# Self attention of a two-layer cross-attention block: scores from four 64x64 tiles, and V, staging and copy of V one place further ahead

## What is computed

```
qkv = x @ w_qkv + b_qkv
q, k, v = jnp.split(qkv, 3, axis=-1)
# mha, per batch and head (Sq = Skv = 56, D_HEAD = 8, 16 heads):
scores = einsum('bhqd,bhkd->bhqk', qh, kh) / sqrt(8)
attn = softmax(scores)
sa = einsum('bhqk,bhkd->bhqd', attn, vh)  @ w_so + b_so
x = layer_norm(x + sa, ln_g, ln_b)
```

## Time and profile before

| | |
|---|---|
| median of 3 runs | 1102.7 us (1102.0 to 1103.2) |
| the profiled execution | 1105.47 us, of which the span in the trace is 1103.7 us |
| busy share of the span | PE 93%, DVE 67%, ACT 51%, POOL 35% |
| mean granted PE clock | 0.96 of full speed |
| self attention, first matmul to the start of the last copy to att | 25.15 to 68.95 us of the span |
| what follows it | barrier, first matmul of the next block at 69.50 us |

### The profile page before, as it was taken

One profiled execution on the slowest core, in us unless ns is written; L12 is line 12 of the kernel. 1 busy time (PEld: TensorE's weight loads), 2 busy tenths in 40 slices (PEclk: granted clock), 3 DMA queues, 4 the chain that ended last, 5 costly groups with the idle time before them and its releaser, 6 DMA issues. The chain is left out here.

```text
span 1103.7 us, 31615 instructions
## 1 busy us (share of the span) xinstructions
PE 1023.4 (93%) x12044; PEld 744.2 (67%) x12044; DVE 743.7 (67%) x1406; ACT 566.9 (51%) x1135; POOL 390.1 (35%) x273
## 2 busy tenths in 40 slices
PE   4975899999999999979688999999999999999997
PEld 2652576777777776745335777787777777777786
DVE  4655778887888878320796767677677676767752
ACT  2442577776776777731345444445444444445542
POOL 4821121111211123030105554546455454555542
PEclk9986899999999999979798999999999999999998
DMA  3502544445444443030021111110111111111100
GB/s 99 143 2 91 144 133 130 134 145 148 132 132 129 146 129 91 2 98 1 1 56 43 57 56 42 51 44 33 54 56 54 47 43 55 35 40 56 35 4 4
DMA packets 47021, 79.90 MB, mean 72 GB/s; under 512 B 6978, under 2 KB 33812, under 8 KB 46964
## 3 DMA queue, kind: packets, MB, share of 16 engines
q1 hardware_dynamic: 46964, 79.10, 24.4%
HBM read 50.93 MB, written 21.96 MB: 66 GB/s over the span
## 5 line engine op out<-in xcount | busy, mean ns | idle before, releaser
L1366 ACT ACTIVATE P<-PS 125x448 f32<-125x448 f32 x384 | 207.1, 544 | 265.7 <-PE PS L1275 263.8
L1256 POOL TENSOR_TENSOR Pl<-P 125x896 f16<-125x896 f32 x128 | 230.0, 1802 | 237.4 <-ACT P L1366 237.4
L1002 DVE TENSOR_REDUCE m<-PS 128x1 f32<-128x500 f32 x336 | 220.7, 674 | 115.3 <-PE PS L993 113.4
L908 DVE TENSOR_REDUCE m_part<-PS 128x1 f32<-128x500 f32 x336 | 210.4, 673 | 60.8 <-PE PS L810 59.4
L1291 PE MATMUL PS<-cNh,P 125*128 125x97 f16 x1344 | 197.9, 208 | 0.1
L1293 PE MATMUL PS<-cNh,Pl 125*128 125x97 f16 x1344 | 197.4, 207 | 0.0
L1292 PE MATMUL PS<-cNl,P 125*128 125x96 f16 x1344 | 196.8, 206 | 0.0
L886 ACT ACTIVATE Pb<-PS 125x448 f32<-125x448 f32 x384 | 185.9, 547 | 20.1 <-PE PS L785 18.7
L1292 PEld LDWEIGHTS PS<-cNl,P 125*128 125x128 bf16 x1344 | 131.8, 98 | 25.4
L810 PE MATMUL PS<-KH,Qmx 128*128 128x500 f16 x336 | 129.7, 388 | 13.9 <-PEq L682 7.8
L1291 PEld LDWEIGHTS PS<-cNh,P 125*128 125x128 bf16 x1344 | 131.2, 98 | 15.7 <-issue 3.2
(11 more groups left out here) (167 smaller groups left out, 1521.9 us busy)
## 6 DMA issues: line engine op xcount, KB each, us to landing
Kst<-k_halves SPq DMA_DIRECT2D x144, 125.0 KB, 2.8
k_halves<-KH SPq DMA_DIRECT2D x16, 750.0 KB, 3.3
cx<-in_ctx SPq DMA_DIRECT2D x16, 562.5 KB
d_cx<-in_ctx SPq DMA_DIRECT2D x16, 562.5 KB
c_halves<-cHi SPq DMA_DIRECT2D x16, 281.2 KB, 2.6
c_halves<-cLo SPq DMA_DIRECT2D x16, 281.2 KB, 3.0
cTh<-c_halves SPq DMA_DIRECT2D x16, 281.2 KB, 3.1
cTl<-c_halves SPq DMA_DIRECT2D x16, 281.2 KB, 4.0
```

What stands on the lines that cost most here:

```text
L908: nc.vector.tensor_reduce(m_part[:, t, part:part + 1], PS[:, 6 + k % 2, 0:SP], AX.X, ALU.max).then_inc(s_reduced, 1)
L1002: nc.vector.tensor_reduce(m21[:, t, part:part + 1], PS[:, S1[k % 2], 0:SP], AX.X, ALU.max).then_inc(n_red, 1)
L1256: nc.gpsimd.tensor_tensor(Pl[:, c % NP], P1[:, c % NP], high, ALU.subtract).then_inc(n_low_p, 1)
L1366: nc.scalar.activation(P1[:, c % NP, half * HALF:(half + 1) * HALF], PS[0:KC, u % 3, 0:HALF], ACT.Exp).then_inc(n_exp, 1)
```

## The change

It has three parts.

1. Scores by halves. Heads 0 to 7 lie in feature rows 0 to 63 and heads 8 to 15 in rows 64 to 127. A half of the heads now uses only its own 64 rows of Qp and of Kbd, so a tile's four score matmuls have 64x64 weights, each in another quarter of PE's array (rows 0 or 64, columns 0 or 64), with the same 448 columns each. Kbd shrinks to 128 rows by 8x56 = 448 columns per batch (the table C_M8 has the mask r % 64 // 8), and has two slots in the same memory, so Kbd of tile t waits for the scores of tile t-2.
2. V one tile further ahead. PE makes V of tile t+1 in step t (`own_values`), in the same place, between the transposes and the product. The waits that stood before the scores of t+1 (staging, Sm of t-1, both batches of Kbd) now stand there, ahead of V of t+1, and nothing is waited for at the scores. DVE copies V2 of t ahead of top of t instead of behind Sm of t.
3. ACT stages t+1 ahead of the two copies to PT of t-1, and now also waits for the scores of t-1.

The core of the diff:

```diff
 TWO_ONES = float(np.array(0x3C003C00, np.uint32).view(np.float32))
-C_ID, C_M4, C_MM, C_M16, C_MV, C_END = 0, 128, 132, 139, 155, 157
+C_ID, C_M4, C_MM, C_M16, C_MV, C_M8, C_END = 0, 128, 132, 139, 155, 157, 165
 def shape_table():
...
     t[:, C_M16:C_MV] = r // DH0 == np.arange(H)
-    t[:, C_MV:C_END] = r // SQ == np.arange(2)
+    t[:, C_MV:C_M8] = r // SQ == np.arange(2)
+    t[:, C_M8:C_END] = r % 64 // DH0 == np.arange(8)
     return t
...
         selfa = ExitStack()
-        Kbd = sb_in(selfa, "Kbd", [D, 2, H, SQ])
+        Kbd = sb_in(selfa, "Kbd", [D, 2, 2, H // 2, SQ])
         Qp = sb_in(selfa, "Qp", [D, 2, 2, 64])
...
                                     spread(tab[:, C_M16:C_MV], 2, SQ), ALU.mult).then_inc(qmx_laid, 1)
-        def lay_own_keys(t, j):
-
-            nc.gpsimd.tensor_tensor(Kbd[:, j], SKT[:, bass.ds(t * 2 + j, 1), :].broadcast_to([D, H, SQ]),
-                                    spread(tab[:, C_M16:C_MV], 2, SQ), ALU.mult).then_inc(s_kbd, 1)
+        def lay_own_keys(t, slot, j):
+
+            nc.gpsimd.tensor_tensor(Kbd[:, slot, j], SKT[:, bass.ds(t * 2 + j, 1), :].broadcast_to([D, H // 2, SQ]),
+                                    spread(tab[:, C_M8:C_END], 2, SQ), ALU.mult).then_inc(s_kbd, 1)
         table_in, x_in, qkv_in, bv_in, wkv_in, later_in = (
...
                 for j in range(2):
-                    lay_own_keys(0, j)
+                    lay_own_keys(0, 0, j)
             @block.tensor
...
                     for j in range(2):
-                        nc.vector.tensor_copy(Vbd[:, slot, j, :, 16:18], spread(tab[0:TP, C_MV:C_END], 1, PAIRS)).then_inc(s_ones, 1)
+                        nc.vector.tensor_copy(Vbd[:, slot, j, :, 16:18], spread(tab[0:TP, C_MV:C_M8], 1, PAIRS)).then_inc(s_ones, 1)
                 split_context(dve, -1, 0, 0, mode=OPEN)
...
                     if there(t, 0) and not (isinstance(t, int) and t == 0):
+                        wait_for(pool, s_scores, t * 2 - 2)
                         for j in range(2):
-                            wait_for(pool, s_scores, t * 2 + j - 1)
-                            lay_own_keys(t, j)
+                            lay_own_keys(t, slot, j)
                     if there(t, -1):
...
                                 V2[:, 1 - slot, j].rearrange("p (a b c) -> p a b c", a=PAIRS, b=2),
-                                spread(spread(tab[0:TP, C_MV:C_END], 1, PAIRS), 3, DH0), ALU.mult)
+                                spread(spread(tab[0:TP, C_MV:C_M8], 1, PAIRS), 3, DH0), ALU.mult)
                         v.then_inc(s_vbd, 1)
...
                                        PS[:, SB, 256:384].rearrange("p (j q) -> p j q", j=2)[:, :, 0:SQ]).then_inc(s_att, 1)
+                    if there(t, 1):
+                        wait_for(act, s_v, t)
+                        wait_for(act, s_scores, t * 2)
+                        stage(t + 1, 1 - slot)
                     if there(t, -1):
...
                             nc.scalar.copy(PT[:, 4 * half:4 * half + 4].rearrange("p b c -> p (b c)"), PS[0:TP, 4 + half, :]).then_inc(s_pt, 1)
-                    if there(t, 1):
-                        wait_for(act, s_v, t)
-                        stage(t + 1, 1 - slot)
                     if there(t, 0):
...
             def _(pe):
+                def own_values(t, slot):
+
+                    pe.wait_ge(s_staged, t * 2 + 2)
+                    wait_for(pe, s_vkept, t)
+                    wait_for(pe, s_sm, t - 1)
+                    pe.wait_ge(s_kbd, t * 2 + 2)
+                    for j in range(2):
+                        mm = pe.matmul(PS[0:TP, 7, j * D:(j + 1) * D], Xd[:, slot, j], wqkv[:, 2 * D:3 * D], start=True, stop=True)
+                    mm.then_inc(s_v, 1)
+
                 def step(t, slot):
...
                     if there(t, 0):
-                        pe.wait_ge(s_staged, t * 2 + 2)
-                        wait_for(pe, s_sm, t - 1)
                         for j in range(2):
-                            pe.wait_ge(s_kbd, t * 2 + j + 1)
                             for half in range(2):
-                                mm = pe.matmul(PS[64 * j:64 * j + 64, 2 * slot + half, 0:HALF], Qp[:, slot, j, :],
-                                               Kbd[:, j, 8 * half:8 * half + 8, :], start=True, stop=True)
+                                rows_of = slice(64 * half, 64 * half + 64)
+                                mm = pe.matmul(PS[64 * j:64 * j + 64, 2 * slot + half, 0:HALF], Qp[rows_of, slot, j, :],
+                                               Kbd[rows_of, slot, j], start=True, stop=True)
                             mm.then_inc(s_scores, 1)
...
                                 mm.then_inc(s_turned, 1)
-                    if there(t, 0):
-                        wait_for(pe, s_vkept, t)
-                        for j in range(2):
-                            mm = pe.matmul(PS[0:TP, 7, j * D:(j + 1) * D], Xd[:, slot, j], wqkv[:, 2 * D:3 * D], start=True, stop=True)
-                        mm.then_inc(s_v, 1)
+                    if there(t, 1):
+                        own_values(t + 1, other)
                     if there(t, -1):
...
                         mm.then_inc(s_pv, 1)
+                own_values(0, 0)
                 over_tiles(pe, step)
...
                     if there(t, 0):
+                        dve.wait_ge(s_v, t + 1)
+                        if isinstance(t, int) and t == 0:
+                            dve.wait_ge(bv_in, 16)
+                        wait_for(dve, s_vbd, t - 1)
+                        nc.vector.tensor_tensor(V2[:, slot], PS[0:TP, 7, 0:2 * D].rearrange("p (j d) -> p j d", j=2),
+                                                spread(rows[:, R_BV, :], 1, 2), ALU.add).then_inc(s_vkept, 1)
                         dve.wait_ge(s_scores, t * 2 + 2)
...
                                                 ALU.subtract).then_inc(s_sm, 1)
-                        dve.wait_ge(s_v, t + 1)
-                        if isinstance(t, int) and t == 0:
-                            dve.wait_ge(bv_in, 16)
-                        wait_for(dve, s_vbd, t - 1)
-                        nc.vector.tensor_tensor(V2[:, slot], PS[0:TP, 7, 0:2 * D].rearrange("p (j d) -> p j d", j=2),
-                                                spread(rows[:, R_BV, :], 1, 2), ALU.add).then_inc(s_vkept, 1)
                     if there(t, -1):
```

## The result

The changed kernel takes 1093.2 us (median of 4 runs, 1091.94 to 1093.83) against 1102.61 before: ratio 0.9909, 95% interval 0.9896 to 0.9923. A later set of 4 runs gave 1092.4 and 0.9911 (0.9896 to 0.9926). Forecast were 7.5 us less, 1095.2, with a range of 1092.6 to 1099.0; measured are 9.4 and 10.3 us less. In the table the stage is the self attention, from its first matmul to the start of the last copy to att; the numbers are of one profiled execution of each kernel.

What follows compares the result with a forecast made beforehand. PE was taken to bound the self attention, late through POOL in every other tile. Head 2.2, middle 3.5 and tail 1.8 us less made 7.5, from the median 1102.7 to 1095.2 us; range 1092.6 to 1099.0.

Steps and rivals of the forecast that it cites:

- PE sets the pace, and is late through POOL in every other tile: Self attention before: PE busy all 9.47 us of two tiles, scores 1.67 or, waiting for Kbd, 2.76; 4.65 a tile.
- Scores from quarters 0.92: Scores on PE: four quarters run beside each other, 0.92 us, 0.75 less than paired, 1.84 less than late.
- Rivals 1 to 3: Scores on PE: row halves take turns, 1101.2, chance 0.09; program order, 1104.2, 0.03; quarters never overlap, 1113.2, 0.02.
- Rival 2: Scores on PE keep program order, no later matmul starting ahead: 2.04 us, total 1104.2; chance 0.03.
- 0.10 for the change of shape: PE, product to scores: the array changes its shape there, adding 0.10 us a tile; bounds 0 and 0.17.
- Kbd 1.67: POOL's Kbd for both batches halves from 3.34 to 1.67 us, with no wait for Kbd on PE.
- The 1096.5: Upper end of the forecast's own range before 0.7 for spread: Kbd's length keeps POOL at 4.1 us a tile.
- What is late next is the staging, 3.95 a tile: ACT's att, Qp, Xd, PT delay V and product: 3.95 us a tile against PE's 3.54; middle 3.5 us less.
- Head 2.2: Start of self attention: scores of tile 2 at 33.75 in place of 35.97, 2.2 us less.
- tail 1.8: Scores of tile 7 to the last copy to att: 7.93 us in place of 9.71, 1.8 less.
- The rest neither gains nor loses: Outside the stage: no gain or loss behind the barrier, and nothing for the table's 8 wider columns.
- Rival 4, the clock: PE idles 0.4 us of 3.95; a low clock for one stretch doubles a tile's 3.5: 1098.7, chance 0.06.

Runs made afterwards that it cites:

- parts 2 and 3 alone: Changed kernel with scores from full rows and the full Kbd in two slots; 1099.1 us, ratio 0.996 to the kernel before.
- the experiment on the first block: Kernel before, with Kbd of tile 0 in four POOL instructions of 448 columns in place of two of 896; 1101.8 us, ratio 0.9989.
- the first part alone: Changed kernel with V, V2 and staging at their old places, loop written out; 1092.78 us (0.9903), again 1093.56 (0.9921), ratios to the kernel before.
- scores twice: Changed kernel with each tile's four score matmuls issued twice, semaphores raised by the second four alone; 1138.8 us.

## Why the prediction was right or wrong

1. *PE sets the pace, and is late through POOL in every other tile.* Right: before, the spacings alternate between 4.2 and 5.3 to 5.5; now they are even, and PE waits for Kbd nowhere.
2. *Scores from quarters 0.92.* Right: 0.92, and 0.75 more when they are doubled. Rivals 1 to 3 are out. Rival 2, a strict order of starts, would have needed five slots of 0.375 and 2.04 us; the eight passes fit in two slots.
3. *0.10 for the change of shape.* The product to the scores takes 1.04 in place of 0.96, so 0.08; with full rows (parts 2 and 3 alone) it is 0.95 again.
4. *Kbd 1.67.* It took 1.83 for both batches, which nothing on PE waits for. (The 1096.5 that stands for a long Kbd comes out at 1096.6: 1095.2, five times 0.15, and 0.7.)
5. *What is late next is the staging, 3.95 a tile.* The mechanism is right: moved back it costs 1.1 us a tile, moved ahead it frees 0.33 and leaves PE's own sum of 3.52, for which I had 3.54. The size was off by 0.10: the copies follow each other in 0.19 and 0.28 where I had 0.25 and 0.35, and then not PT but V is last, 0.43 behind Xd and 0.62 before the product. The five spacings of the middle gave 4.15 us less for the 3.5 of the sum.
6. *Head 2.2 (to the scores of tile 2), tail 1.8 (behind those of tile 7).* 2.08 and 1.78.
7. *The rest neither gains nor loses.* This step failed: the sum put what lies outside the stage at nothing. I had read no row of the first block, though POOL's Kbd of tile 0, which the change shortens, stands in it. That block ended 1.4 us earlier. Of this 0.75 is the DVE instruction beside POOL's, shown by the experiment on the first block; 0.53 was there before POOL's first Kbd began (18.47 and 17.94), and two profiles of before differ there by as much (18.47 and 17.95); 0.1 is left. What follows the barrier took 3.4 us less in two profiles of either kernel, with 8 us less at the low clock on it; since the same kernel differed there by up to 2.8, whether any of this comes from the change stays open. The medians hold only a part of it, as 9.4 less 8.0 and 0.75 leaves 0.6, or 1.5 by the second set.
8. *Rival 4, the clock.* Not in the changed kernel, where PE idles 0.3 us a tile. In five profiles of its neighbours 3 to 20 us at the low clock fell on the stage from 24 to 30 us on, later than its own; why it falls where it does is not shown.

The sum was thus low by 0.5 in the stage and by about 1.4 to 2.3 outside it, of which 0.75 is shown to be the change's.

## What to carry to other kernels

When an edit shortens an instruction, follow each place where that instruction is issued, in other blocks too, and ask which engine it holds up there. A step that is moved ahead for one engine's sake (V here) pulls what it waits for onto the path; order the supplying engine's work by who waits for it first. Try each part of a change alone: two parts of this one make the stage about 2 us longer than the first part alone has it. Gains of 1 or 2 us in one stage may not be seen at the end while the rest differs by 2 to 3 us between two executions of one kernel; and before a difference far from the edit is put down to the edit, profile each kernel more than once.

## What the runs showed of the hardware

**A DVE instruction with two SBUF inputs did not end before the POOL instruction beside it.** It took 1.67 us beside one of 1.74, and 0.92 beside one of 0.99; each time it started 0.35 behind POOL's and ended 0.28 behind POOL's end. The Trainium skill says as much: SBUF — State Buffer, Who interferes with whom, has such an instruction share its second read port with GpSimd, and the one issued first keep it. The profiles of before, of the changed kernel and of the experiment on the first block agree; what the DVE instruction takes with POOL idle no run shows.

**Four quarters of the array run beside each other in fp32**: the scores take 0.92 us where the two column halves took 1.67, and 1.67 again when they are doubled.

**The length of a block of code can cost far away.** With scores twice, PE stands idle in the loop of the last stage, once in each of five rounds, before the first matmul of line 1283 (the scores there). From the view of PE's waits, 640 to 1000 us (what it stood before, what ended it, then total us, times, longest):

```profile
PE PS L1283 <- issue: 24.8, 5, 5.6
```

The idle time is followed by a stretch at the low clock, here behind 708 us in the busy time by stretch:

```profile
703.50:708.20 4.70, 0.20 (x5) 0.04 (x2) 1.17 (x4) 0.00 (x0) 0.00 (x0) 1.00 0.46 108
708.20:715.00 6.80, 6.73 (x18) 3.94 (x19) 1.36 (x2) 2.17 (x4) 2.60 (x2) 0.50 0.02 5
```

and the DMA queue that carries instructions moved more (the page's part on queues: packets, MB, share), first the changed kernel, then this one:

```profile
q8 instruction: 40, 0.66, 0.3%
```

```profile
q8 instruction: 85, 1.39, 0.5%
```

That is 45 packets more, with the code of the loop unchanged and more code ahead of it; from 640 to 1000 us it is 45 packets against 6. Behind the barrier this kernel took 1072.2 us, some 42 more than the changed one. The idle time of 24.8 and half of five stretches of 6.8 us at the low clock make 41.8, an estimate that agrees. The Trainium skill, Runtime: NRT & Kernel Launch, Instruction fetch mechanics, says that a taken branch whose target lies outside the loaded window waits for a fetch by DMA. The trace agrees with the fetches and with the wait; that it is where the loop lies in memory that decides was not tried by itself. All other kernels here kept 40 packets.
